# A Perceiver block on one core: first two text key tiles by plain products, bias rows in one pass, image part and last rescalings on GpSimd, last output in two pieces

## Chip, cores and metric

One core of one Trainium2 chip runs the whole block as one program. The metric is the device time of one execution in microseconds (us); smaller is better.

## What is computed

128 latent rows of width 512 go through three stages: cross attention over 12,544 context rows, self attention (16 heads of 128, weights given as 4-bit codes with scales), and a mixture of experts (2 shared, 32 routed, all computed). Only the cross attention is touched. Cut to what matters:

```python
xq = _layernorm(x)
q = rms_norm(linear(xq, q_w, q_b), norm_q_w)                 # 16 heads of 32
k_img, v_img = rms_norm(linear(ctx[:257], k_img_w, k_img_b), norm_k_img_w), linear(ctx[:257], v_img_w, v_img_b)
k_txt, v_txt = rms_norm(linear(ctx[257:], k_w, k_b), norm_k_w), linear(ctx[257:], v_w, v_b)
att = attention(q, k_img, v_img) + attention(q, k_txt, v_txt)
x1 = x + linear(att, o_w, o_b)
```

(The first lines are a summary in the reference's own function names.)

## The kernel before

**Tiling.** Keys come in tiles of 128. Group 0 is the image: 257 keys in three tiles (its last tile starts at the last image key). The text keys from 256 on make groups 1 to 24 of 512 keys, four tiles or two *pairs* each. The work runs in steps s = 0 to 26, each of 16 slots h (one per head). In step s the scores, maxima, exponentials, transposes and value products of group s-1 are interleaved with the key and value products of the next keys: slots 0 to 7 compute the second pair of group s, slots 8 to 15 the first pair of group s+1. Step 0 has the image's products (`image`) and slots 8 to 15 only.

**Products of text keys.** A pair of tiles times the K and V weights is a 2 by 2 block product. It is done with seven block products (Strassen-Winograd, `NPOS = 7`), not eight: POOL forms sums of key blocks (`first_sums`, `third_sum`, `fourth_sum`, L549 to L562) and the sums of weight blocks once (L514 to L524), and every operand is split into a high part that the one-pass float32r format holds and the low rest (`split_first`, `split`, L569 to L580 on POOL; for weights `split_weight`, high part on ACT L656 to L667, low part on DVE L924). Each block product is six one-pass matmuls of 512 columns (hi·hi, hi·lo, lo·hi for two chunks), so a pair costs 42 on PE (L1354). DVE and ACT take the sums out of PSUM. The image tiles use the plain form: 12 matmuls for a tile and a weight (L1245).

**Order.** Each engine has one queue, in the order of the code; nothing is scheduled at run time. `steps` runs each engine's `step` function. PE's score product in slot h waits for ACT's exponential of slot h-2 (`e_exp`, two score banks). ACT's `scale_keys(s, 1)` stands in slot 1 of its queue ahead of the exponential of slot 2, and waits for POOL's `key_norm(s, 1)` (L480, L482), which POOL's queue has behind all blocks of the step before and the next `first_sums(0)`. SP issues the loads, and `stack`: 12 DMAs that put transposed keys of eight heads into `k_stack`. The memset of `p_tail` on POOL waits for the eighth low weight part (`e_wlo`).

**Start.** PE spreads six bias and norm rows over 128 partitions, each by a float32 product of a row of ones with the row (L1250), four ahead of the transposes of the normalised x and two behind them; then the query product (L1264), then the image.

**End.** Steps 25 and 26 only drain (`draining`). DVE holds two running outputs, `o_st[0]` of the image and `o_st[1]` of the text. In step 24 it normalises the image's part (L987, L989) and adds two bias rows (L991, twice). In slot 12 of steps 3 to 25 it rescales `o_st[1]` (L1107), and in slot 14 adds the newest output (L1115). In step 26 ACT copies the 512 columns of the last output from PSUM (L795), PE transposes them back, DVE scales and adds (L1104, L1105, L1112, L1113), PE transposes the sum, ACT copies it (L839), and PE multiplies it with the output weight (L1437).

```python
if end and h == (5 if s >= NG else 4):
    eng.wait_ge(e_pv, (s - 2) * (NH // HC) + NH // HC)
```

## Time and profile before

| | us |
|---|---|
| median of 3 runs | 1240.7 (1240.31 to 1241.61) |
| the profiled execution | 1240.53 |
| its span, first to last instruction | 1238.8 |
| busy PE | 1186.9 (96%) |
| busy PE weight loads | 928.5 (75%) |
| busy DVE | 951.4 (77%) |
| busy ACT | 825.4 (67%) |
| busy POOL | 761.6 (61%) |

PE is TensorE, PEld its weight loads, DVE VectorE, ACT ScalarE, POOL GpSimd, SP the queue that issues DMAs. Times in rows are us from the span's start; L12 is line 12 of the kernel. A timeline row gives start, length, engine, line, operation, output <- inputs, shapes, count, and in brackets the idle time before it and what ended it. PE's matmuls overlap, so the distance of two starts is what one costs, not the length shown. PEclk is the TensorE clock granted, as a share of full speed.

### The profile page before, as it was taken

The numbers are of one execution on the slowest core, as the hardware profiler recorded it, in microseconds if no ns is written. First come the engines' busy times: TensorE is split into PE (matmuls) and PEld (weight loads), VectorE is DVE, ScalarE is ACT, GpSimd is POOL, SyncE is SP. The second block draws the span as 40 slices with busy tenths as digits, with TensorE's granted clock in tenths as the row PEclk, the third lists the DMA queues.
The fourth block names the chain that finished last, engine by engine and source line by source line (L and its number), as shares of the span: only waits on it lengthen the run. The fifth ranks groups of instructions, "written<-read, shape, count | busy, mean of one in ns | idle before, by whom it ended". The sixth has DMA issues, their size and how long they took to land.

```text
span 1238.8 us, 26287 instructions
## 1 busy us (share of the span) xinstructions
PE 1186.9 (96%) x8740; PEld 928.5 (75%) x8740; DVE 951.4 (77%) x1647; ACT 825.4 (67%) x1828; POOL 761.6 (61%) x1071
## 2 busy tenths in 40 slices
PE   8779999999999999999999999999998779899998
PEld 4557887887888788887878887887787535488886
DVE  3648888788888888887887887888877823399997
ACT  4547767777676777677767767776777713377775
POOL 5988787778787787877787877888772000000000
PEclk9989999999999999999999999999999999999999
DMA  6125866666766667656667666676653999359990
GB/s 237 31 73 137 214 166 171 163 168 187 187 171 165 170 163 213 173 161 173 171 177 195 173 162 172 156 209 174 171 136 94 290 392 362 153 222 358 363 369 21
DMA packets 132390, 236.74 MB, mean 191 GB/s; under 512 B 18081, under 2 KB 45217, under 8 KB 131873
## 3 DMA queue, kind: packets, MB, share of 16 engines
q1 hardware_dynamic: 132258, 235.06, 64.4%
q8 instruction: 73, 1.20, 0.4%
q14 instruction: 59, 0.48, 0.1%
HBM read 140.87 MB, written 17.04 MB: 127 GB/s over the span
## 4 chain that ended last, share of the span: by engine, by line
PE 82%; DVE 9%; POOL 4%; issue 3%; ACT 1%; DMA 0%; POOLq 0%; SPq 0%; DVEq 0%; ACTq 0%
PE ps L1354 31%; PE ps L1237 17%; PE ps L1420 8%; PE ps L1380 8%; PE ps L1452 3%; DVE small L1058 3%; PE ps L1532 3%; PE ps L1535 3%; PE ps L1538 3%; DVE v_second L1041 2%; DVE kt_lo L948 2%; PE ps L1553 1%; PE ps L1561 1%; PE ps L1557 1%; PE ps L1509 1%
## 5 line engine op out<-in xcount | busy, mean ns | idle before, releaser
L1354 PE MATMUL ps<-w_text,cx_blocks 128*128 128x512 f32 x2016 | 548.8, 398 | 4.5 <-ACT u_sb L773 2.0
L1354 PEld LDWEIGHTS ps<-w_text,cx_blocks 128*128 128x128 f32 x2016 | 375.0, 190 | 71.6 <-issue 4.2
L783 ACT ACTIVATE p<-ps,small 128x512 f32<-128x512 f32 (+2 forms) x400 | 271.3, 678 | 210.7 <-DVE small L1060 206.5
L1058 DVE TENSOR_REDUCE small<-ps 128x1 f32<-128x512 f32 (+2 forms) x400 | 270.7, 677 | 129.2 <-PE ps L1380 128.8
L1237 PE MATMUL ps<-ident,p 128*128 128x128 f32 x1584 | 239.7, 273 | 8.9 <-DVE pt L1051 6.9
L1237 PEld LDWEIGHTS ps<-ident,p 128*128 128x128 f32 x1584 | 194.0, 140 | 64.1 <-issue 12.7
L1380 PE MATMUL ps<-k_stack,q_stack 96*128 96x512 f32 (+1 forms) x400 | 192.1, 481 | 7.7 <-ACT p L783 7.7
L765 ACT ACTIVATE pt<-ps 128x512 f32<-128x512 f32 (+1 forms) x250 | 147.6, 590 | 11.4 <-PE ps L1237 7.0
L580 POOL TENSOR_TENSOR cx_blocks<-cx_sum,cx_blocks 128x256 fp32r<-128x256 f32 x192 | 141.7, 738 | 15.1
L578 POOL TENSOR_TENSOR cx_blocks<-cx_sum,small 128x256 fp32r<-128x256 f32 x192 | 119.6, 623 | 45.6 <-PE ps L1354 37.7
L1060 DVE TENSOR_TENSOR small<-small 128x1 f32<-128x1 f32 x400 | 130.3, 326 | 13.7
L1051 DVE COPY pt<-ps 128x512 f32<-128x512 f32 (+1 forms) x150 | 101.4, 676 | 2.2 <-PE ps L1237 2.2
L1380 PEld LDWEIGHTS ps<-k_stack,q_stack 96*128 96x128 f32 x400 | 75.7, 190 | 28.0 <-issue 20.2
L569 POOL TENSOR_TENSOR cx_blocks<-cx,small 128x512 fp32r<-128x512 f32 x48 | 51.4, 1072 | 71.7 <-PE ps L1354 71.7
L948 DVE TENSOR_TENSOR kt_lo<-ps,kt_hi 128x512 fp32r<-128x512 f32 x99 | 67.5, 682 | 27.3 <-ACT kt_hi L706 27.3
L1158 DVE TENSOR_TENSOR w_lo<-expert,w_hi 128x2048 fp32r<-128x2048 f32 x34 | 77.8, 2290 | 11.7 <-ACT w_hi L869 11.6
L701 ACT ACTIVATE kb<-kb,small 128x512 f32<-128x512 f32 x99 | 70.5, 713 | 23.7 <-POOL small L482 23.6
L490 POOL TENSOR_TENSOR codes<-codes,code_scale 128x512 f32<-128x512 f32 x64 | 82.4, 1287 | 0.1
L783 ACT ACTIVATION_READ_ACCUMULATOR p<-ps,small 128x1 f32 x400 | 77.6, 194 | 0.0
L706 ACT ACTIVATE kt_hi<-ps 128x512 fp32r<-128x512 f32 x99 | 58.9, 595 | 27.7 <-PE ps L1237 27.5
L1237 PEld LDWEIGHTS ps<-ident,kb 128*128 128x128 f32 x396 | 47.0, 141 | 31.3 <-issue 18.5
L1237 PE MATMUL ps<-ident,kb 128*128 128x128 f32 x396 | 60.6, 276 | 10.3 <-DVE kt_lo L948 6.7
(218 smaller groups left out, 1861.0 us busy)
## 6 DMA issues: line engine op xcount, KB each, us to landing
expert<-experts SPq DMA_DIRECT2D x34, 1536.0 KB, 8.6
k_stack<-kt_hi SPq DMA_DIRECT2D x384, 128.0 KB, 2.4
cx<-ctx_t SPq DMA_DIRECT2D x48, 512.0 KB, 4.2
k_stack<-kt_lo SPq DMA_DIRECT2D x192, 128.0 KB, 2.4
codes<-codes SPq DMA_DIRECT2D x64, 256.0 KB
code_scale<-code_scales SPq DMA_DIRECT2D x256, 64.0 KB
scaled<-codes SPq DMA_DIRECT2D x64, 256.0 KB, 4.3
weight_q<-scaled SPq DMA_DIRECT2D x1, 4096.0 KB, 14.2
```

The costliest lines, as they stand in the source:

```text
L578: eng.tensor_tensor(block(i, 0), of, ones.broadcast_to((P, CD, P)), ALU.mult).then_inc(e_ahi, 1)
L580: eng.tensor_tensor(block(i, 1), of, block(i, 0).bitcast(F32), ALU.subtract).then_inc(e_ab, 1)
L765: eng.activation(pt_sb[hp % NPT][:, 0:n], ps_pt[hp % 2][:, 0:n], copy).then_inc(e_pta, 1)
L783: eng.activation(pb[:, lo:hi], score_bank(s, h)[:, lo:hi], exp, bias=nm[1 - par][:, h:h + 1], accum_out=ls[1 - par][:, h:h + 1]).then_inc( ...
L948: eng.tensor_tensor(kt_lo[:, :, part], ps_t[:, :].rearrange("p (c k) -> p c k", c=DC), kt_hi[:, :, part].bitcast(F32), ALU.subtract).then_ ...
L1051: eng.tensor_copy(pt_sb[hp % NPT][:, 0:n], ps_pt[hp % 2][:, 0:n]).then_inc(e_pte, 1)
L1058: eng.tensor_reduce(ngm[:, h:h + 1], score_bank(s, h)[:, lo:hi], AX.X, ALU.max, negate=True).then_inc(e_gm, 1)
L1060: eng.tensor_tensor(nm[1 - par][:, h:h + 1], ngm[:, h:h + 1], old[:, h:h + 1], ALU.min).then_inc(e_nm, 1)
L1237: last = eng.transpose(dst[:, c * P:(c + 1) * P], src[:, c * P:(c + 1) * P], ident[:, :])
L1354: last = eng.matmul(ps_a[(p + i + 1) % 2][:, :], blk[:, i, a, c * P:(c + 1) * P], w_t[:, i, w, c * D:(c + 1) * D], start=(i in FRESH and c ...
L1380: eng.matmul(score_bank(s, h)[:, 0:n], q_st[qi][0:NST * HD, h, :], stk[0:NST * HD, h, 0:n], start=True, stop=True).then_inc(e_qk, 1)
L1420: last = eng.matmul(ps_o[jp * HD:(jp + 1) * HD, c * P:(c + 1) * P], vb[k][:, head * HD:(head + 1) * HD], pt_sb[head % NPT][:, k * P:(k + 1 ...
```

## The change

1. **Rows at the start.** The six rows lie on six partitions. POOL makes a selector of 6 by 768, ACT and DVE split the rows in high and low, and PE spreads each row by two one-pass matmuls. Three rows go ahead of the query product and three behind it. The layer norm no longer waits for the first image tile.
2. **First pair of text keys.** It is computed plainly: POOL makes only a high and a low part of the 256 keys (`pair_hi`, `pair_lo`), PE does four products of 12 matmuls (48 in place of 42). Step 0 is `image` alone, with no slots; POOL leaves out the pair's sums and seven block splits. Weights are split in another order, the two that the plain values need first (raw blocks `b12`, `b22`), and the last of nine in slot 0 of step 1. The loads of the next keys go ahead of `stack(0, True)` on SP.
3. **End.** POOL takes the image part's scaling and two additions and the rescalings of steps 24 and 25. In steps 25 and 26 ACT's copy moves from slot 5 to slot 7. The last output goes through as 384 and 128 columns.

POOL's queue from the last image split on, where the first text pair and the key norms of the image stand (`cx` are the loaded keys, `cx_sum` their sums, `cx_blocks` the split blocks, `w_sum` and `stage_k`, `stage_v` the weights, `first_pair` the new high and low part). Before:

```order
L506 TENSOR_SCALAR small<-small 128x1 [waits q_squared]
L509 TENSOR_TENSOR small<-small 128x1 [waits pool_init]
L549 TENSOR_TENSOR cx_sum_88<-cx 128x256 [waits keys_loaded0]
L553 TENSOR_TENSOR cx_sum_89<-cx_sum_88,cx 128x256 [waits key_sums]
L480 TENSOR_TENSOR small<-small 128x1 [waits k_squared]
L482 TENSOR_TENSOR small<-small 128x1 [waits k_mean_square]
L569 TENSOR_TENSOR cx_blocks<-cx,small 128x2x256
L571 TENSOR_TENSOR cx_blocks<-cx,cx_blocks 128x2x256 [waits block_hi]
L480 TENSOR_TENSOR small<-small 128x1 [waits k_squared]
L482 TENSOR_TENSOR small<-small 128x1 [waits k_mean_square]
L514 TENSOR_TENSOR w_sum_58<-stage_v,stage_k 128x1024 [waits w_loaded_v,w_loaded_k]
```

and now:

```order
L517 TENSOR_TENSOR first_pair_91<-cx,small 128x1024 [waits cx_lo,keys_loaded0]
L519 TENSOR_SCALAR small<-small 128x1 [waits q_squared]
L522 TENSOR_TENSOR small<-small 128x1 [waits pool_init]
L525 TENSOR_TENSOR first_pair_92<-cx,first_pair_91 128x1024 [waits block_hi]
L489 TENSOR_TENSOR small<-small 128x1 [waits k_squared]
L491 TENSOR_TENSOR small<-small 128x1 [waits k_mean_square]
L489 TENSOR_TENSOR small<-small 128x1 [waits k_squared]
L491 TENSOR_TENSOR small<-small 128x1 [waits k_mean_square]
L530 TENSOR_TENSOR w_sum_58<-stage_v,stage_k 128x1024 [waits w_loaded_v,w_loaded_k]
```

The two sums and two splits of the first pair are gone from between the query's and the key norms; one split of 1024 columns stands ahead of the query's two operations and one behind them. Behind the weight sums (L514 to L524, now L530 to L536 and L549) the second pair follows at once.

PE's queue behind the second transposes of the queries (L1274 before, L1349 now), up to the first score product. Before:

```order
L1274 MATMUL ps<-ident,q_thrice_121 96x128 x15
L1354 MATMUL ps<-w_text,cx_blocks 128x512 [waits v_stored,w_lo_split,block_split]
L1354 MATMUL ps<-w_text,cx_blocks 128x512 x5
L1354 MATMUL ps<-w_text,cx_blocks 128x512 [waits v_stored,w_lo_split,block_split]
L1354 MATMUL ps<-w_text,cx_blocks 128x512 x5
L1354 MATMUL ps<-w_text,cx_blocks 128x512 [waits first_product_biased,w_lo_split,block_split]
L1354 MATMUL ps<-w_text,cx_blocks 128x512 x5
L1354 MATMUL ps<-w_text,cx_blocks 128x512 [waits k_biased,w_lo_split,block_split]
L1354 MATMUL ps<-w_text,cx_blocks 128x512 x5
```

and now (each of the four products is 12 matmuls):

```order
L1349 MATMUL ps<-ident,q_thrice_126 96x128 x15
L1318 MATMUL ps<-w_text,first_pair_91 128x512 [waits v_stored,w_lo_split,block_split]
L1318 MATMUL ps<-w_text,first_pair_91 128x512
L1318 MATMUL ps<-w_text,first_pair_92 128x512
L1318 MATMUL ps<-w_text,first_pair_91 128x512 x2
L1318 MATMUL ps<-w_text,first_pair_92 128x512
L1318 MATMUL ps<-w_text,first_pair_91 128x512 x2
L1318 MATMUL ps<-w_text,first_pair_92 128x512
L1318 MATMUL ps<-w_text,first_pair_91 128x512 x2
L1318 MATMUL ps<-w_text,first_pair_92 128x512
L1318 MATMUL ps<-w_text,first_pair_91 128x512 [waits v_stored,w_lo_split]
```

The block product that waited for sums, copies and `block_split` is replaced by plain ones that wait for the low weight parts, `v_stored` and `k_biased`; the seven block products of the second pair follow, each still waiting for `block_split`.

DVE's queue in step 24, slots 12 to 14 (`small` holds maxima and sums, `o_st_111` is the image's output, `o_st_112` the text's; 116 and 117 now). Before:

```order
L1095 TENSOR_TENSOR small<-small 128x16 [waits o_added,l_added,alpha]
L1098 TENSOR_TENSOR small<-small 128x16 [waits l_scaled,exp]
L1107 TENSOR_TENSOR o_st_112<-o_st_112,small 128x512
L1058 TENSOR_REDUCE small<-ps 128x1 [waits scores]
L1060 TENSOR_TENSOR small<-small 128x1 [waits group_max]
L991 TENSOR_TENSOR o_st_111<-o_st_111,o_rows 128x512
L1058 TENSOR_REDUCE small<-ps 128x1 [waits scores,dve_chain]
L1060 TENSOR_TENSOR small<-small 128x1 [waits group_max]
L1051 COPY pt_102<-ps 128x512 [waits pv_batch,p_transposed]
L1115 TENSOR_TENSOR o_st_112<-ps,o_st_112 128x512 [waits o_scaled,o_transposed]
```

and now:

```order
L1119 COPY pt_105<-ps 128x512 [waits pv_batch,p_transposed]
L1161 TENSOR_TENSOR small<-small 128x16 [waits o_added,l_added,alpha]
L1164 TENSOR_TENSOR small<-small 128x16 [waits l_scaled,exp]
L1126 TENSOR_REDUCE small<-ps 128x1 [waits scores]
L1128 TENSOR_TENSOR small<-small 128x1 [waits group_max]
L1126 TENSOR_REDUCE small<-ps 128x1 [waits scores]
L1128 TENSOR_TENSOR small<-small 128x1 [waits group_max]
L1119 COPY pt_107<-ps 128x512 [waits pv_batch,p_transposed]
L1188 TENSOR_TENSOR o_st_117<-ps,o_st_117 128x512 [waits o_scaled,o_transposed]
```

The rescaling and one of the two bias additions between the maxima are gone from DVE; in POOL's queue they follow the last key norm. The addition of the newest output still waits for `o_scaled`.

The diff, cut to its core:

```diff
-                if s == 0:
-                    eng.wait_ge(e_klo, GT)
-                    eng.wait_ge(e_vp, GT)
-                    stack(0, True)
...
+                if s == 0:
+                    eng.wait_ge(e_klo, GT)
+                    eng.wait_ge(e_vp, GT)
+                    stack(0, True)
...
-            eng.memset(ones_row[:, :], 1.0).then_inc(e_pool, 1)
+            sel = row_ones[:, :, :]
+            eng.memset(sel, 0.0).then_inc(e_pool, 1)
             eng.memset(ident[:, :], 0.0).then_inc(e_pool, 1)
             eng.wait_ge(e_pool, 2)
+            eng.affine_select(out=sel, in_=sel, compare_op=ALU.not_equal, fill=1.0,
+                              base=0, pattern=[[-1, NROW], [0, P]], channel_multiplier=1).then_inc(e_pool, 1)
...
+                keys = cx[:, :, 0:2 * P]
+                eng.wait_ge(e_c[0], 16)
+                eng.wait_ge(e_clo, GT)
+                eng.tensor_tensor(pair_hi[:, :, :], keys, ones.broadcast_to((P, DC, 2 * P)), ALU.mult).then_inc(e_ahi, 1)
                 eng.wait_ge(e_qsq, 1)
...
+                eng.wait_ge(e_ahi, 1)
+                eng.tensor_tensor(pair_lo[:, :, :], keys, pair_hi[:, :, :].bitcast(F32), ALU.subtract).then_inc(e_ab, NPOS)
+                key_norm(0, 0, 1)
+                key_norm(0, 1, 1)
...
+            def image_part():
+                eng.wait_ge(e_orows, 48)
+                eng.wait_ge(e_irl, 1)
+                o3 = o_st[0][:, :].rearrange("p (h d) -> p h d", h=NH)
+                eng.tensor_tensor(o3, o3, rl.unsqueeze(2).broadcast_to((P, NH, HD)), ALU.mult).then_inc(e_img, 1)
+                for i in (1, 2):
+                    eng.wait_ge(e_img, i)
+                    eng.tensor_tensor(o_st[0][:, :], o_st[0][:, :], o_rows[:, i, :], ALU.add).then_inc(e_img, 1)
+
+            def last_weight_sum():
+                eng.wait_ge(e_wlo, 4)
+                eng.tensor_tensor(b12, b22, b12, ALU.subtract).then_inc(e_tt, 1)
...
-                if nxt:
+                strass = nxt and s > 0
+                if strass:
                     first_sums(0)
-                if s == 0:
-                    key_norm(0, 0, 1)
...
-                if nxt:
+                if strass:
                     split_first(0)
-                if s == 0:
...
+                    if s == 0:
+                        last_weight_sum()
                     split(1, 2, sum_y[:, :, :], 2)
-                    key_norm(s + 1, 0, 1)
+                    if s > 0:
+                        key_norm(s + 1, 0, 1)
...
+                    if s == 0:
+                        key_norm(1, 0, 1)
+                        eng.wait_ge(e_wlo, 8)
+                        eng.memset(p_tail, 0.0).then_inc(e_pz, 1)
                     split(1, 6, quarter(1, 1, 1), 0)
+                if s == NG - 1:
+                    image_part()
+                if s in (NG - 1, NG):
+                    eng.wait_ge(e_al, s - 1)
+                    eng.wait_ge(e_oadd, s - 2)
+                    o3 = o_st[1][:, :].rearrange("p (h d) -> p h d", h=NH)
+                    eng.tensor_tensor(o3, o3, al.unsqueeze(2).broadcast_to((P, NH, HD)), ALU.mult).then_inc(e_osc, 1)
```

```diff
-                        eng.wait_ge(e_qp, 1)
-                    eng.activation(w_t[:, i - 1, 0, :], (t2[:, :, :], t1[:, :, :], b12, b22, b21)[i - 3].rearrange("p c o -> p (c o)"),
+                    if i == 8:
+                        eng.wait_ge(e_pp, NPOS)
+                    if i > 4:
+                        eng.wait_ge(e_tt, (2, 1, 4, 3)[i - 5])
+                    eng.activation(w_t[:, W_SLOT[i - 3], 0, :], (b12, b22, t2[:, :, :], t1[:, :, :], b12, b21)[i - 3].rearrange("p c o -> p (c o)"),
...
-            for i in range(4):
-                store_row(i)
+            eng.wait_ge(e_pool, 4)
+            eng.activation(row_sel[:, :, :], row_ones[:, :, :], copy).then_inc(e_rowh, 1)
...
+            eng.activation(row_hi[:, :], row_sb[:, :], copy).then_inc(e_rowh, 1)
+            store_row(0)
+            store_row(1)
...
+            def plain_values(j):
+
+                eng.wait_ge(*((e_pp, NPOS) if j else (e_vp, GT + 1)))
+                eng.activation(v_first[1][j][:, :], ps_a[0][:, :], copy).then_inc(e_v, 1)
...
                     image()
+                    plain_values(0)
+                    square_keys(1, 0, 1)
+                    plain_values(1)
+                    scale_keys(1, 0, 1)
+                    split_weight(8)
+                    return
...
-                    if end and h == (5 if s >= NG else 4):
-                        eng.wait_ge(e_pv, (s - 2) * (NH // HC) + NH // HC)
...
+                        if s <= NG:
+                            eng.activation(ot_sb[:, :], ps_o[:, :], copy).then_inc(e_oc, 1)
+                        else:
+                            eng.activation(ot_sb[:, 0:TA], ps_o[:, 0:TA], copy).then_inc(e_oc, 1)
+                            eng.wait_ge(e_pv, NG * (NH // HC))
+                            eng.activation(ot_sb[:, TA:], ps_s[0][:, 0:P], copy).then_inc(e_oc, 1)
```

```diff
-                    if not loop and s == NG - 1:
-                        image_part(h)
+                    if s == NG - 1 and h == 8:
+                        eng.reciprocal(rl, l_st[0]).then_inc(e_irl, 1)
...
-                        else:
+                        elif s < NG - 1:
                             eng.tensor_tensor(o3, o3, al.unsqueeze(2).broadcast_to((P, NH, HD)), ALU.mult).then_inc(e_osc, 1)
...
+                            for i, (src, part) in enumerate(((ps_t[:, 0:TA], slice(0, TA)), (ps_s[1][:, 0:P], slice(TA, D)))):
+                                n = (part.stop - part.start) // HD
+                                heads = rl[:, part.start // HD:part.stop // HD].unsqueeze(2).broadcast_to((P, n, HD))
+                                dst = o_st[0][:, part]
+                                eng.wait_ge(e_ot, NG + i)
+                                chain(eng.tensor_tensor(dst.rearrange("p (h d) -> p h d", h=n), src.rearrange("p (h d) -> p h d", h=n),
+                                                        heads, ALU.mult))
+                                eng.tensor_tensor(dst, dst, o_st[1][:, part], ALU.add).then_inc(e_osum, 1)
...
-                eng.matmul(ROW_BANKS[i][:, :], ones_row[:, :], row_sb[:, i * D:(i + 1) * D], start=True, stop=True).then_inc(e_row, 1)
...
+                eng.matmul(ROW_BANKS[i][:, :], row_sel[:, i, :], row_hi[:, :], start=True, stop=False)
+                eng.matmul(ROW_BANKS[i][:, :], row_sel[:, i, :], row_lo[:, :], start=False, stop=True).then_inc(e_row, 1)
+
+            eng.wait_ge(e_pool, 4)
+            eng.wait_ge(e_rowh, 2)
+            eng.wait_ge(e_rowo, 1)
+            spread_row(0)
+            spread_row(1)
...
+            spread_row(2)
...
+            for i in range(3, NROW):
+                spread_row(i)
...
+                eng.wait_ge(e_ab, NPOS)
+                for j in range(2):
+                    keys = slice(j * P, (j + 1) * P)
+                    a = [(pair_hi[:, c, keys], pair_lo[:, c, keys]) for c in range(DC)]
+                    for of, at in (("k", (0, 1)), ("v", (6, 5))):
+                        eng.wait_ge(e_wlo, 3 if of == "k" else 5)
+                        if of == "k":
+                            eng.wait_ge(*((e_kb, GT + 1) if j else (e_v, 2)))
+                        else:
+                            eng.wait_ge(e_v, GT + j)
+                        w = [(w_t[:, at[c // CD], 0, c % CD * D:(c % CD + 1) * D],
+                              w_t[:, at[c // CD], 1, c % CD * D:(c % CD + 1) * D]) for c in range(DC)]
+                        last = split_product(ps_a[of == "k"][:, :], a, w, 0, 3 * DC)
+                        if of == "k" or j == 0:
+                            last.then_inc(e_kp if of == "k" else e_vp, 1)
+                last.then_inc(e_pp, NPOS)
...
+                    if s == 1 and p < 0 and i in (2, 3, 4, 6):
+                        eng.wait_ge(e_wlo, 9 if i == 6 else i + 4)
...
+                        into = ps_s[0][:, 0:P] if s == NG + 1 and c == TA // P else ps_o[:, c * P:(c + 1) * P]
+                        if s == NG + 1 and c == TA // P:
+                            eng.wait_ge(e_oc, NG)
+                            transposes(ps_t, ot_sb, TA // P).then_inc(e_ot, 1)
...
+                    if end and h == 12 and s == NG + 1:
+                        eng.wait_ge(e_oc, NG + 1)
+                        eng.transpose(ps_s[1][:, 0:P], ot_sb[:, TA:], ident[:, :]).then_inc(e_ot, 1)
...
-            transposes(ps_t, o_st[0]).then_inc(e_at, 1)
-            eng.wait_ge(e_atc, 1)
+            transposes(ps_t, o_st[0], TA // P).then_inc(e_at, 1)
+            eng.wait_ge(e_osum, 2)
+            eng.transpose(ps_s[0][:, 0:P], o_st[0][:, TA:], ident[:, :]).then_inc(e_at, 1)
...
+                eng.wait_ge(e_atc, 1 if c < TA // P else 2)
```

## Rows read from the trace of the kernel before

**Rows 1.** Stretches: length, busy (count) of PE PEld DVE ACT POOL; PEclk, DMA, GB/s
```profile
20.00:70.00 50.00, 41.19 (x195) 31.47 (x193) 34.38 (x42) 23.73 (x44) 44.44 (x43) 1.00 0.22 60
70.00:80.00 10.00, 3.06 (x10) 2.62 (x11) 1.42 (x4) 4.44 (x13) 9.36 (x15) 0.59 0.16 52
80.00:90.00 10.00, 10.00 (x75) 8.04 (x73) 6.46 (x15) 6.21 (x17) 8.47 (x14) 0.90 0.02 3
```

**Rows 2.** Timeline of PE, first and fifth score product of step 1
```profile
61.52 0.28 PE L1380 MATMUL ps<-k_stack,q_stack 96*128 96x258 f32 x1
...
76.94 0.58 PE L1380 MATMUL ps<-k_stack,q_stack 96*128 96x258 f32 x1 [7.21 <-ACT p L783]
```

**Rows 3.** Timeline of ACT, the operation that held PE
```profile
75.10 0.72 ACT L701 ACTIVATE kb<-kb,small 128x512 f32<-128x512 f32 x1 [8.28 <-POOL small L482]
```

**Rows 4.** Timeline of POOL, from the query's scale to the key norm of step 1
```profile
23.45 1.40 POOL L506 TENSOR_SCALAR small<-small 128x1 f32<-128x1 f32 x1 [6.35 <-ACT q_sq L721]
...
25.46 0.74 POOL L549 TENSOR_TENSOR cx_sum<-cx 128x256 f32<-128x256 f32 x1
...
32.81 2.55 POOL L514 TENSOR_TENSOR w_sum<-stage_v,stage_k 128x1024 f32<-128x1024 f32 x1
...
35.65 2.62 POOL L482 TENSOR_TENSOR small<-small 128x1 f32<-128x1 f32 x1
...
64.49 0.95 POOL L622 MEMSET p_tail<- 128x1020 f32 x1
...
74.52 0.55 POOL L482 TENSOR_TENSOR small<-small 128x1 f32<-128x1 f32 x1
```

**Rows 5.** POOL's work on tile cx_blocks, 25.4 to 59.9 us: length, busy (count)
```profile
25.40:59.90 34.50, 13.06 (x12) 1.00 0.10 24
```

**Rows 6.** Groups of POOL there, the sums: count | busy us, mean ns | idle before
```profile
L553 POOL TENSOR_TENSOR cx_sum<-cx_sum,cx 128x256 f32<-128x256 f32 x2 | 1.8, 902 | 0.2
L562 POOL TENSOR_TENSOR cx_sum<-cx,cx_sum 128x256 f32<-128x256 f32 x1 | 1.7, 1719 | 0.0
L558 POOL TENSOR_TENSOR cx_sum<-cx 128x256 f32<-128x256 f32 x1 | 1.6, 1605 | 0.1
```

**Rows 7.** Timeline of DVE, the low part of the text key weights
```profile
35.58 2.28 DVE L924 TENSOR_TENSOR w_text<-stage_k,w_text 128x2048 fp32r<-128x2048 f32 x1
```

**Rows 8.** Timeline of PE, from rows and query product to second query transposes
```profile
3.89 7.16 PE L1250 MATMUL ps<-rows,ones_row 1*128 1x512 f32 x8 [3.89 <-DMA rows<-first_rows]
...
15.74 6.07 PE L1264 MATMUL ps<-wq,pt 128*128 128x512 f32 x8
21.25 0.80 PE L1245 MATMUL ps<-w_hi_k_img,img_cx_hi 128*128 128x512 f32 x1
...
29.84 0.60 PE L1237 MATMUL ps<-ident,kb 128*128 128x128 f32 x4
...
45.09 1.91 PE L1274 MATMUL ps<-ident,q_thrice 128*96 128x128 f32 x16
```

**Rows 9.** Timeline of SP, the issue of the first weight
```profile
2.60 0.51 SPq L320 DMA_DIRECT2D stage_k_img<-k_img_wt  x1
```

**Rows 10.** DMA issues, the same load: KB, us from issue to landing
```profile
stage_k_img<-k_img_wt SPq DMA_DIRECT2D x1, 1024.0 KB, 8.2
```

**Rows 11.** Timeline of DVE, step 24: one that goes, two that stay
```profile
957.02 0.68 DVE L989 TENSOR_TENSOR o_st<-o_st,small 128x512 f32<-128x512 f32 x1
...
968.36 0.68 DVE L1058 TENSOR_REDUCE small<-ps 128x1 f32<-128x512 f32 x1
969.08 0.74 DVE L1060 TENSOR_TENSOR small<-small 128x1 f32<-128x1 f32 x1
```

**Rows 12.** Timeline of POOL, its one addition in that stretch
```profile
968.52 1.28 POOL L634 TENSOR_TENSOR x_again<-x_again,o_rows 128x512 f32<-128x512 f32 x1 [14.63 <-DMA x_again<-x]
```

**Rows 13.** Timeline of DVE, the last sum
```profile
996.91 0.69 DVE L1113 TENSOR_TENSOR o_st<-o_st,o_st 128x512 f32<-128x512 f32 x1
```

**Rows 14.** Timeline of PE, the output product
```profile
999.00 3.70 PE L1437 MATMUL ps<-wo,kb 128*128 128x512 f32 x8 [0.69 <-ACT kb L839]
```

185 lines of the change are left out of this document (94 added, 91 removed).

## Prediction

> **What bounds the kernel now.** I read the page first (PE busy for 96% of the span), then the chain of waits, then the busy time in stretches, then the timelines of the stretches where PE is not full. Three quarters of the execution is steps 1 to 24 with PE always busy; the change leaves them alone, so they only move. What it can win lies in the first 80 us, in the drain (steps 24 to 26) and in the last output.
>
> At the start one place stands out. PE issues the first score product of step 1 at 61.52 and the fifth at 76.94, after 7.21 us of idleness [rows 2]. It waits for ACT's exponential, ACT stands in its queue at the key scaling of step 1, and that has waited 8.28 us for POOL's key norm [rows 3], whose last operation starts at 74.52 [rows 4]. POOL is busy for 9.36 of 10 us there while PE has 3.06 [rows 1]. So POOL's queue sets when step 1 can go on, and the length of that queue is what the change cuts. The idle PE also loses its clock: granted 0.59 in 70 to 80 us and 0.90 in 80 to 90 us [rows 1].
>
> **POOL's queue.** Removed for the first pair: 12 instructions on the blocks, 13.06 us [rows 5], and the four sums of 0.74, 0.90, 1.60 and 1.72 us [rows 4, 6], 18.0 us together; with some 0.07 us between neighbours 19 us. Added: high and low part of 1024 columns. The nearest row from above is a weight sum of 1024 columns, 2.55 us [rows 4]; from below twice nothing, if both fall into idle time. The high part stands in the 6.35 us in which POOL waited for the query [rows 4] and is free; I take 2.5 us for the low part. The query is squared earlier (below), so the scaling that started at 23.45 starts at about 19, 4.3 us earlier. Sum: 74.5 - 19 - 4.3 + 2.5 = 53.7 for the last key norm, were POOL's queue all there is. It now also waits: the memset of `p_tail` stands behind the eighth low weight part on DVE. Behind the memset come its own 0.95 us [rows 4], one split (1.4), two sums (1.6) and the norm (0.8), for which see the next paragraph.
>
> **PE's own queue becomes the bound.** Rows at the start: eight records of 7.16 us [rows 8] ahead of the transposes, and two rows more behind them, turn into four one-pass matmuls ahead, two behind and six after the query product. A one-pass matmul of 512 columns costs 8.59 / 36 = 0.24 us (36 of them from 21.25 to 29.84 [rows 8]), so 12 cost 2.9 us. The new work ahead of it is not shown by any row: POOL makes a selector of 768 columns on six partitions twice, ACT and DVE copy and subtract. By the memset of 1020 columns at 0.95 [rows 4] this is 0.7 us for each of POOL's two, at most 1.7 for the selection, and 1 to 2 us on ACT and DVE; I put the rows at 6.6 and the query product at 9.9, not 15.74 [rows 8]. It takes 5.5 us (15.74 to 21.25), three rows 1.4 us: image products from 16.8. The other bound of that moment is the first weight: issued at 2.60, 8.2 us to landing [rows 9, 10], so 10.8, then 1.8 us on ACT and 2.3 us on DVE (2048 columns take 2.28 [rows 7]): 15.0. So 16.8, between 15.2 and 17.8, where it was 21.25.
>
> From there PE has 36 + 36 image and 48 plain matmuls (six more than the pair's 42, 1.4 us of PE), that is 120 x 0.24 = 28.7 us, three groups of key transposes at 0.44 (29.84, four of them), and two of 16 query transposes at 1.9 at most [rows 8]: 33.8 us. That gives 50.6; for the waits that are left (third key tile, which needs ACT, POOL and DVE in turn) 0.4: step 1 starts at 51.0 instead of 61.52. Slots 0 to 3 took 76.94 - 7.21 - 61.52 = 8.2 us [rows 2]; they have a ninth weight split on ACT and DVE beside them now. So the fifth score product is at 59.2.
>
> POOL is then not late: the eighth low part follows DVE's use of the third plain product (48.1), at 50.5; memset, split, sums and norm make 55.1, or 56.7 if DVE's ninth split holds POOL up; ACT's scaling, squares and exponential then allow the fifth product at 57.2 to 58.8. The two paths are within 2 us, which is why I don't count on less than 59. The 12 DMAs of the second `stack` may start at 51 and are needed by ACT in slot 5, some 10 us later: covered, with 1 us to spare.
>
> The fifth product moves from 76.94 to 59.2: **17.7 us**. And PE, now without a gap of 7 us, keeps the full clock. The clock has two levels, 1.2 and 2.4 GHz; a mean of 0.59 is 8.2 us at the lower, with nearly all of PE's 3.06 us in it, and 0.90 is 2 us [rows 1]. Half of that work time is lost: 1.5 + 1.0; I take **2.3 us**.
>
> **Drain.** In step 24 DVE is busy without pause. It loses one scaling, two additions and a rescaling, in step 25 another rescaling, 0.68 us each [rows 11]: 3.4 us. POOL has the time: its only work there is one addition of 1.28 us [rows 12], so four make 5.3 us from slot 8, and the addition of slot 14 finds its rescaling ready. But POOL's work costs DVE something. DVE's minimum of two one-column operands takes 0.16 us at 968.36 and 0.74 at 969.08 [rows 11], when POOL's addition ran from 968.52 to 969.80 [rows 12]: it ended with it. Such a minimum stands behind every maximum. Five new POOL operations at 0.58 us each: 2.9 us back. Net 0.5.
>
> The Trainium skill (SBUF — State Buffer, the part on the shared port pair) says that a DVE instruction with two SBUF inputs and a GpSimd instruction that reads SBUF exclude each other for their whole length. The row at 969.08 agrees; taken at its worst, every POOL operation would hold DVE for all of its length, which is a rival below.
>
> ACT's copy in slot 7 instead of 5 lets two exponentials of step 25 go first: 0.3.
>
> **Last output.** The first 384 columns go ahead, but DVE reaches them only after the same work as before, so the first sum ends at about 997.1, not 997.6 (996.91 + 0.69 [rows 13]). Transposes and copy of three quarters are each 0.1 to 0.2 shorter, and the last quarter hides behind the first three chunks of the product. That starts at 998.3 instead of 999.00 [rows 14]: 0.7. Nothing later changes.
>
> **Sum.** 17.7 + 2.3 + 0.5 + 0.3 + 0.7 = 21.5 us. Against the profiled execution (1240.53, span 1238.8) this gives 1219.0; the median of the runs is 1240.7, so the two bases are one for this purpose. A measurement of this kernel can tell 0.2%, 2.5 us, from no change.
>
> **Rivals.**
> 1. *POOL stays the bound.* For it: a sum of 256 columns took 0.74 us alone and 1.60 and 1.72 beside DVE's splits [rows 4, 6], a norm 2.62 beside a split from 35.58 [rows 4, 7]. If five operations more are stretched by 0.9, the fifth product is at 63.7: 1223.5. Against it: DVE's splits then fall where POOL would wait anyway. Chance 0.20.
> 2. *No cost on DVE, fewer waits.* The weight bounds the image at 15.2, the third key tile costs nothing, and the drain gives the whole 3.4 us: 1.6 + 2.4 = 4 us more, 1215. Chance 0.20.
> 3. *POOL holds DVE at its worst in the drain.* Five operations at 1.28 are 6.4 us against 3.4: 3.5 us worse than my 0.5, 1222.5. Chance 0.07.
> 4. *Slower: PE runs the new start at 1.2 GHz.* At half clock each us of PE time loses half a us; the 21.5 us are gone when 43 us of the start, nearly all of 17 to 60, run so. Then 120 matmuls and the transposes cost 34 us more: 1253. Against it: from 20 to 70 us the granted clock was 1.00, with PE idle for 9 of the 50 us [rows 1]. Chance 0.02.
> 5. *The POOL stop was not what held step 1*, the weights' low parts were, and the ninth comes no earlier than the last did: within 0.2%. Against it: 8.28 us at one wait [rows 3]. Chance 0.01.
>
> The forecast itself has 0.50. Its range, with start and end bounds, is 1216 to 1222; to hold eight in ten I reach to rivals 1 to 3 and some way beyond: 1213 to 1225. Faster by over 0.2%: 0.97; within: 0.01; slower: 0.02.
>
> **What would show it.** Image products start near 17; step 1's first score near 51 and its fifth near 59; the granted clock stays at 1 from 10 to 90 us; DVE's minima in step 24 average over 0.4 us; the output product starts 0.7 us closer to the last value product. I am wrong if ACT's key scaling of step 1 again waits over 3 us for POOL, if PE's steps 1 to 23 get another length, or if the drain from step 24 on changes by over 3 us.

## The result, and the profile after

The changed kernel takes 1229.24 us, the median of 4 runs (1228.29 to 1230.93), the kernel before 1241.15 us beside it: ratio 0.990, 95% interval 0.9886 to 0.9913. That is 11.9 us faster. Forecast were 1219.0 us and a range of 1213 to 1225: the sign is right, the gain is half of what was forecast, and the time lies outside the range. The profiled execution took 1228.65 us, its span 1226.9, so it can be compared with the one before (1240.53, 1238.8).

Where TensorE's timeline stands at the same instruction in both:

| instruction | before | after | won so far |
|---|---|---|---|
| first score product of step 1 | 61.52 | 59.17 | 2.35 |
| fifth score product of step 1 | 76.94 | 68.85 | 8.09 |
| first of step 2 | 103.96 | 95.25 | 8.71 |
| first of step 24 | 952.95 | 944.74 | 8.21 |
| last value product | 994.16 | 984.55 | 9.61 |
| output product | 999.00 | 988.45 | 10.55 |
| first expert product | 1084.00 | 1073.17 | 10.83 |
| last product | 1234.96 | 1223.08 | 11.88 |

The stretches that answer to [rows 1], same columns:

```profile
20.00:70.00 50.00, 41.16 (x195) 32.66 (x194) 36.53 (x41) 28.07 (x53) 46.97 (x42) 0.97 0.27 76
70.00:80.00 10.00, 9.91 (x78) 7.75 (x76) 6.96 (x16) 7.34 (x20) 9.16 (x15) 1.00 0.03 10
80.00:90.00 10.00, 8.87 (x70) 6.69 (x69) 6.10 (x14) 6.09 (x17) 6.64 (x11) 1.00 0.48 121
```

The hole of 70 to 80 us is gone, and the clock is 1.00 there. But POOL is busy for 46.97 of the 50 us from 20 on, more than before, although 16 instructions of the first pair have left its queue and only two have come. TensorE's timeline says where the early lead went (first image product, first key transposes, then the first and the fifth score, which answer to [rows 2]):

```profile
17.79 0.50 PE L1318 MATMUL ps<-w_hi_k_img,img_cx_hi 128*128 128x512 f32 x1 [0.30 <-DVE w_lo_k_img L983]
...
31.29 1.05 PE L1310 MATMUL ps<-ident,kb 128*128 128x128 f32 x4 [4.98 <-ACT kb L739]
32.14 3.20 PE L1349 MATMUL ps<-ident,q_thrice 128*96 128x128 f32 x16
...
59.17 0.28 PE L1473 MATMUL ps<-k_stack,q_stack 96*128 96x258 f32 x1
...
68.85 0.39 PE L1473 MATMUL ps<-k_stack,q_stack 96*128 96x258 f32 x1 [0.52 <-ACT p L835]
```

The image products start 3.5 us earlier than before, yet the first key transposes start 1.5 us later (29.84 before [rows 8]), after a wait of 4.98 us, and the 16 query transposes behind them take 3.20 instead of 1.91 us: the clock had gone down to its lower level (granted 0.83 on the mean of 30 to 40 us, 1.00 before). The cause stands in the timelines of POOL and DVE:

```profile
14.54 1.04 POOL L511 TENSOR_TENSOR img_cx_hi<-img_cx,small 128x512 fp32r<-128x512 f32 x1 [5.70 <-DMA img_cx<-ctx_t]
15.66 3.22 POOL L513 TENSOR_TENSOR img_cx_lo<-img_cx,img_cx_hi 128x512 fp32r<-128x512 f32 x1
18.85 1.03 POOL L511 TENSOR_TENSOR img_cx_hi<-img_cx,small 128x512 fp32r<-128x512 f32 x1
20.03 3.16 POOL L513 TENSOR_TENSOR img_cx_lo<-img_cx,img_cx_hi 128x512 fp32r<-128x512 f32 x1
23.33 1.89 POOL L517 TENSOR_TENSOR first_pair<-cx,small 128x1024 fp32r<-128x1024 f32 x1
25.31 0.19 POOL L519 TENSOR_SCALAR small<-small 128x1 f32<-128x1 f32 x1
25.59 0.56 POOL L522 TENSOR_TENSOR small<-small 128x1 f32<-128x1 f32 x1
26.10 2.34 POOL L525 TENSOR_TENSOR first_pair<-cx,first_pair 128x1024 fp32r<-128x1024 f32 x1
...
66.15 0.20 POOL L489 TENSOR_TENSOR small<-small 128x1 f32<-128x1 f32 x1
66.43 0.55 POOL L491 TENSOR_TENSOR small<-small 128x1 f32<-128x1 f32 x1
```

```profile
15.00 2.73 DVE L983 TENSOR_TENSOR w_lo_k_img<-stage_k_img,w_hi_k_img 128x2048 fp32r<-128x2048 f32 x1 [7.28 <-ACT w_hi_k_img L686]
...
19.16 2.88 DVE L983 TENSOR_TENSOR w_lo_v_img<-stage_v_img,w_hi_v_img 128x2048 fp32r<-128x2048 f32 x1 [0.83 <-ACT w_hi_v_img L686]
21.96 0.68 DVE L1020 TENSOR_TENSOR kb<-ps,k_bias 128x512 f32<-128x512 f32 x1
```

The image's low parts took POOL 1.26 us before and take 3.22 and 3.16 now: the first weights are ready sooner, so DVE's low parts fall on them. POOL is through with the image at 23.2, then makes the pair's high part, and the query's scale, which was to start at 19, starts at 25.31. The norm that the fifth score needs starts at 66.15; it was 74.25 before. The fifth score stands 2.7 us behind this start in both. The sign that I had named for a POOL that is still the bound did not come, though: ScalarE's key scaling waits 1.00 us for POOL, not over 3.

```profile
67.01 0.73 ACT L739 ACTIVATE kb<-kb,small 128x512 f32<-128x512 f32 x1 [1.00 <-POOL small L491]
```

That wait is short because TensorE and ScalarE are late themselves: the first score of step 1 stands at 59.17 and not at 51.0.

### The profile page after: what moved, and what is told of

Same layout as the page of the kernel before. It is cut to its first block, busy times and chain, and to the rows that moved or that the text cites. A ratio compares the mean times of both kernels' runs of the same rounds, so it can differ in the third digit from the quotient of the medians.

```text
span 1226.9 us, 26290 instructions
## 1 busy us (share of the span) xinstructions
PE 1179.2 (96%) x8746; PEld 925.8 (75%) x8746; DVE 954.3 (78%) x1643; ACT 827.7 (67%) x1833; POOL 764.6 (62%) x1063
## 4 chain that ended last, share of the span: by engine, by line
PE 80%; DVE 9%; POOL 5%; issue 3%; DMA 1%; ACT 1%; SPq 0%; POOLq 0%; DVEq 0%; ACTq 0%
PE ps L1447 31%; PE ps L1310 16%; PE ps L1517 8%; PE ps L1473 8%; PE ps L1554 4%; DVE small L1126 3%; PE ps L1634 3%; PE ps L1637 3%; PE ps L1640 3%; DVE v_second L1109 2%; DVE kt_lo L1012 2%; PE ps L1655 1%; PE ps L1663 1%; PE ps L1659 1%; PE ps L1611 1%
## 5 line engine op out<-in xcount | busy, mean ns | idle before, releaser
L1447 PE MATMUL ps<-w_text,cx_blocks 128*128 128x512 f32 x1974 | 536.8, 397 | 1.3 <-ACT v_first L792 0.7
L1447 PEld LDWEIGHTS ps<-w_text,cx_blocks 128*128 128x128 f32 x1974 | 366.4, 189 | 65.7 <-issue 2.7
L605 POOL TENSOR_TENSOR cx_blocks<-cx_sum,cx_blocks 128x256 fp32r<-128x256 f32 x188 | 138.8, 738 | 14.8
L1128 DVE TENSOR_TENSOR small<-small 128x1 f32<-128x1 f32 x400 | 132.8, 332 | 13.7
L1012 DVE TENSOR_TENSOR kt_lo<-ps,kt_hi 128x512 fp32r<-128x512 f32 x99 | 67.5, 682 | 25.4 <-ACT kt_hi L744 25.2
```

Of the source, the lines that this page charges most:

```text
L605: eng.tensor_tensor(block(i, 1), of, block(i, 0).bitcast(F32), ALU.subtract).then_inc(e_ab, 1)
L1012: eng.tensor_tensor(kt_lo[:, :, part], ps_t[:, :].rearrange("p (c k) -> p c k", c=DC), kt_hi[:, :, part].bitcast(F32), ALU.subtract).then_ ...
L1128: eng.tensor_tensor(nm[1 - par][:, h:h + 1], ngm[:, h:h + 1], old[:, h:h + 1], ALU.min).then_inc(e_nm, 1)
L1447: last = eng.matmul(ps_a[(p + i + 1) % 2][:, :], blk[:, i, a, c * P:(c + 1) * P], w_t[:, i, w, c * D:(c + 1) * D], start=(i in FRESH and c ...
```

## The experiments

There are two theories for the 9.6 us that the start fell short (fifth score at 68.85, forecast 59.2). **Order**: instructions of the first pair stand ahead of the query's scale and the key norms. **Turns**: GpSimd's instructions and DVE's instructions with two SBUF inputs run one after the other, so only their sum counts. One measure serves throughout, the **chain**: from POOL's start on the second image tile (14.54 above) to the start of that norm (66.15), 51.6 us; it was 61.9 before (12.31 to 74.25). Each run below has one profile. How far the chain can be trusted is shown by the six profiles whose start is that of the changed kernel (the changed kernel, 1, 11, 12, 14, 15): 51.6 or 51.7 us in all six. In the two with the old start it is 61.9 and 60.9 (before, 2).

**1. The start alone** (image part, rescalings, last output and copy as before):

```diff
-                if s == NG - 1:
-                    image_part()
-                if s in (NG - 1, NG):
...
+                    if not loop and s == NG - 1:
+                        image_part(h)
```

> The changed kernel with its end as before: image part and last rescalings back on DVE, the last output in one piece, ACT's copy back in slot 5. Theory: the parts add, and the start alone is worth what the trace shows between the first scores and step 24 (8.2 us, first score of step 24 at 952.95 before and 944.74 after). So 1241.2 - 8.2 = 1233.0, within 1 us, with the fifth score of step 1 near 68.9. Rival: the start is worth less by itself because the later clock return ahead of the experts (1.5 us at 1075 in the changed kernel) came with it or not by chance; then 1231.5 to 1233. If the drain terms had no worth at all it would be 1229.2.

1232.70 us, ratio 0.9923 (0.9903 to 0.9944), fifth score at 68.21, chain 51.7. By the ratio the start is worth 9.6 us (7.0 to 12.1); by this trace against the one before 8.7 at the fifth score and 9.3 at the first score of step 2. It is most of the gain.

**2. The end alone**, on the kernel before (the same lines the other way round):

> The kernel before with only the end of the change: image part and last rescalings on GpSimd, the last output in two pieces, ACT's copy in slot 7. Theory from the two traces: drain 1.4 us and last output 0.9 us, 2.3 us in all: 1238.8. My recorded forecast for these parts was 0.5 + 0.3 + 0.7 = 1.5: 1239.6. Rival, that the clock's earlier return ahead of the experts belongs to the new end and not to chance: 3.7 us, 1237.4. Rival, GpSimd holds DVE at its worst: no faster than 1241.

1240.02 us, ratio 0.9984 (0.9972 to 0.9996): 2.0 us (0.5 to 3.5). Start and end, 9.6 and 2.0, add to what the whole change gives, 11.9. But this trace has neither the short drain nor the early clock of the changed kernel's profiled execution: 40.96 us from step 24's first score to the last value product, against 39.81.

**3. and 4. Another order in GpSimd's queue.** In 3 the query's scale goes ahead of the pair's high part; in 4 the first key norm does too, and the second ahead of the low part:

```diff
-                eng.tensor_tensor(pair_hi[:, :, :], keys, ones.broadcast_to((P, DC, 2 * P)), ALU.mult).then_inc(e_ahi, 1)
                 eng.wait_ge(e_qsq, 1)
...
+                key_norm(0, 0, 1)
+                eng.tensor_tensor(pair_hi[:, :, :], keys, ones.broadcast_to((P, DC, 2 * P)), ALU.mult).then_inc(e_ahi, 1)
+                key_norm(0, 1, 1)
                 eng.wait_ge(e_ahi, 1)
```

> The changed kernel with the query's scale ahead of the pair's high part in GpSimd's queue, nothing else. Theory 'order': the scale starts at 23.3 instead of 25.31, DVE's normed query and the image's second and third key sums go 2 us earlier, but the first key norm stays behind the pair's low part at 28.4, so the first key transposes gain only the 0.9 us of ACT's squares; the second and third gain about 2: step 1's first score 1 to 2 us earlier, 1227.5 to 1228.2 against 1229.2. Rival 'GpSimd is full': it is busy from 14.5 to 60.9 but for 0.94 us, so an exchange within it moves nothing: 1229.2.

> The changed kernel with query scale, then first key norm, then the pair's high part, second key norm, and the pair's low part after it. Theory 'order': first key norm at about 24.7, first key transposes at 26 to 27 instead of 31.29, PE without its 4.98 us gap and without the fall of the clock to 0.83 in 30 to 40 us; step 1's first score 3 to 5 us earlier (54 to 56), whole time 1224.5 to 1226.5. Rival 'GpSimd is full': the first score comes earlier but the fifth stays at 68 to 69, because the splits of the second pair and the norm of step 1 stand at the end of GpSimd's queue: 1229.

1230.87 us (0.9915, 0.9895 to 0.9934) and 1231.09 us (0.991, 0.9893 to 0.9927). In 4 the wait that I took for the culprit is gone:

```profile
26.57 0.63 PE L1309 MATMUL ps<-ident,kb 128*128 128x128 f32 x4
...
31.30 0.63 PE L1309 MATMUL ps<-ident,kb 128*128 128x128 f32 x4 [2.35 <-DVE kt_lo L1011]
...
38.89 0.63 PE L1309 MATMUL ps<-ident,kb 128*128 128x128 f32 x4 [4.20 <-DVE kt_lo L1011]
```

TensorE reaches these transposes 4.7 us earlier and without a wait, and then waits 2.35 and 4.20 us for the next key tiles. The fifth score is at 68.24 (68.39 in 3), the chain is 51.7 (51.8): nothing won, since the second image tile was also taken up 0.6 us earlier than in the changed kernel. The theory of the order falls.

**5. More of GpSimd's work**: the pair's high part twice.

```diff
+                eng.tensor_tensor(pair_hi[:, :, :], keys, ones.broadcast_to((P, DC, 2 * P)), ALU.mult).then_inc(e_again, 1)
+                eng.wait_ge(e_again, 1)
                 eng.tensor_tensor(pair_hi[:, :, :], keys, ones.broadcast_to((P, DC, 2 * P)), ALU.mult).then_inc(e_ahi, 1)
```

> The changed kernel with the high part of the first pair made twice on GpSimd, one after the other (1024 columns, 1.89 us in the changed kernel); nothing else. Theory 'GpSimd is full': it is busy from 14.5 to 60.9, so the second copy moves the key norm that the fifth score of step 1 waits for, and this score, by 1.9 us: 51.6 us from the start of the second image tile's high part to that norm become 53.5, and the time 1231.1 against 1229.2. Rival 'the fifth score is bound by TensorE's own products, or by the weights' low parts on DVE': no change, 1229.2.

1230.73 us (0.9906, 0.9891 to 0.9921). Chain 53.6: two us longer, as the turns want. The fifth score itself is at 68.91, where it was, because POOL took up the second image tile at 12.58, two us earlier than in the changed kernel's profile. Only the chain shows the effect; the times differ by less than their intervals.

**6. Less of it**: query and norms first, the pair's high part no longer on GpSimd but on ScalarE, behind the first key squares.

```diff
                 square_keys(0, *IMAGE_TILES[0])
+                eng.activation(pair_hi[:, :, :], cx[:, :, 0:2 * P], copy).then_inc(e_ahi, 1)
                 eng.wait_ge(e_sq, 1)
```

> Like the experiment with the norms first, but the pair's high part made by ScalarE behind the first key squares (1024 columns there take 1.06 us), so GpSimd loses an instruction that took 1.89 us in the changed kernel and 3.49 us with the norms first. Theory 'GpSimd is full': the fifth score of step 1 comes 2 to 3.5 us earlier, 51.6 us from the second image tile to the norm become 48 to 49.7, the time 1226 to 1227.5. Rival 'TensorE or DVE is next': the fifth score moves by less than 1 us.

1227.41 us (0.9876, 0.9859 to 0.9892). Chain 49.7, fifth score at 66.78.

**7. The image's columns ahead of the first weight** in SP's queue:

```diff
+            eng.dma_start(img_cx[:, :, P:IT * P], cxt[:, :, P:IT * P]).then_inc(e_cx, 16)
             load_weight(0)
-            eng.dma_start(img_cx[:, :, P:IT * P], cxt[:, :, P:IT * P]).then_inc(e_cx, 16)
```

> The changed kernel with the rest of the image's columns loaded ahead of the first weight (one DMA issue moved up by one). GpSimd's second image tile starts at 14.5 in the changed kernel, when these columns land; they now land about 2.5 us earlier, the first weight 1.3 us later. Theory 'GpSimd is full and its chain starts with this landing': the chain starts near 12, and the two low parts of 3.2 us lie ahead of DVE's first low part and take 1.3: GpSimd done with the image near 17.5 instead of 23.2, then held by the query's squares at 20 to 21; the fifth score 2 to 4 us earlier, 1225 to 1227. Rival 'the first weight is the start of the chain': everything 1.3 us later, 1230.5.

POOL starts on the second tile at 9.93, and the fifth score is at 64.29, 4.6 us earlier. ScalarE takes up the first weight at 12.65, within the scatter of the other runs. The chain is 51.7 again. That is strange at first: the image's low parts take 1.26 us now, so 3.9 us of stretch are gone, and POOL waited 2.13 us for a load. The two engines show why the sum stays (DVE, then POOL):

```profile
17.40 3.48 DVE L983 TENSOR_TENSOR w_lo_v_img<-stage_v_img,w_hi_v_img 128x2048 fp32r<-128x2048 f32 x1
...
21.61 2.89 DVE L1029 SCALAR_TENSOR_TENSOR q_normed<-q_biased,small,q_rows 128x512 f32<-128x512 f32 x1
```

```profile
16.85 1.89 POOL L517 TENSOR_TENSOR first_pair<-cx,small 128x1024 fp32r<-128x1024 f32 x1 [2.13 <-DMA cx<-ctx_t]
18.82 2.11 POOL L519 TENSOR_SCALAR small<-small 128x1 f32<-128x1 f32 x1
21.02 0.56 POOL L522 TENSOR_TENSOR small<-small 128x1 f32<-128x1 f32 x1
21.54 2.41 POOL L525 TENSOR_TENSOR first_pair<-cx,first_pair 128x1024 fp32r<-128x1024 f32 x1
```

DVE's instruction starts at 17.40, stands until POOL's ends at 18.74, and then needs 2.14 us; POOL's next, of 0.19 us, stands until DVE's ends at 20.88; DVE's `q_normed`, 0.74 us where nothing runs beside it, ends 0.5 us behind the 2.41 us of POOL's low part. Neither runs slowly: each waits for the whole of the other. The measured time was 1230.45 us (0.9898, 0.9882 to 0.9915), no better than the changed kernel: see 11 and 13.

**8. Image columns first, with 6's order and high part on ScalarE:**

```diff
+            eng.dma_start(img_cx[:, :, P:IT * P], cxt[:, :, P:IT * P]).then_inc(e_cx, 16)
             load_weight(0)
...
                 square_keys(0, *IMAGE_TILES[0])
+                eng.activation(pair_hi[:, :, :], cx[:, :, 0:2 * P], copy).then_inc(e_ahi, 1)
```

> Both: image columns ahead of the first weight, query scale and key norms ahead of the pair's parts, the high part on ScalarE. If GpSimd's queue is the bound in both, the gains add: 4 to 7 us, 1222 to 1225. If TensorE's queue takes over (120 products of 0.24 us and 5.1 us of transposes from 19 on give a first score near 53), the first score is at 53 to 55, the fifth at 62 to 64, 1223 to 1224. Rival 'DVE's low parts take over', eight of 1024 columns behind ScalarE: less than 2 us, over 1227.

1227.60 us (0.9884, 0.9869 to 0.9898), fifth score at 65.09, later than in 7. The gains do not add: with less work GpSimd now waits, 3.70 us for the squares of the query and 2.08 and 1.14 for those of the keys, and the chain is 52.2. The turns bind only while both engines have work.

**9. More of DVE's work and none of GpSimd's**: the low part of the third weight twice, at a place where DVE waits anyway. This is the run that tells turns from a full queue.

```diff
+                if i == 2:
+                    eng.tensor_tensor(dst, whole, high.bitcast(F32), ALU.subtract).then_inc(e_again, 1)
+                    eng.wait_ge(e_again, 1)
                 eng.tensor_tensor(dst, whole, high.bitcast(F32), ALU.subtract).then_inc(e_wlo, 1)
```

> The changed kernel with the low part of the third weight (2048 columns, 2.3 us when nothing else runs) made twice on DVE, one after the other, at 34 us, where DVE then waits 2.08 us for ScalarE; GpSimd's instructions are untouched. Theory 'GpSimd and DVE take turns': GpSimd's instructions alone (34.4 us at their shortest) and DVE's with two SBUF inputs (18.2 us) add to the 51.6 us from the second image tile to the key norm of step 1, so 2.3 us more on DVE make 53.9 of 51.6, the fifth score comes 2.3 us later after the landing, time 1231.5. Rival 'only GpSimd's own queue counts' or DVE's idle time takes it: 51.6 stays, 1229.2.

1231.92 us (0.9922, 0.9907 to 0.9937), chain 53.5. DVE and POOL around it:

```profile
31.82 2.59 DVE L984 TENSOR_TENSOR w_text<-stage_k,w_text 128x2048 fp32r<-128x2048 f32 x1
34.44 2.29 DVE L986 TENSOR_TENSOR w_text<-stage_k,w_text 128x2048 fp32r<-128x2048 f32 x1
38.47 0.69 DVE L1015 TENSOR_TENSOR kt_lo<-ps,kt_hi 128x512 fp32r<-128x512 f32 x1 [1.74 <-ACT kt_hi L744]
```

```profile
32.22 2.24 POOL L489 TENSOR_TENSOR small<-small 128x1 f32<-128x1 f32 x1
34.60 2.54 POOL L491 TENSOR_TENSOR small<-small 128x1 f32<-128x1 f32 x1
```

DVE still waits 1.74 us afterwards, so its own queue had room for the second low part; POOL's step of 0.55 us takes 2.54. The 2.3 us that DVE got lengthen the chain by 1.9. As in 5, the fifth score is where it was, at 68.61, because the chain began two us earlier (12.39).

**10. The better start**: image columns first, the high part on ScalarE right behind the second image weight.

```diff
                 split_weight(1)
+                eng.wait_ge(e_clo, GT)
+                eng.wait_ge(e_c[0], 16)
+                eng.activation(pair_hi[:, :, :], cx[:, :, 0:2 * P], copy).then_inc(e_ahi, 1)
                 eng.wait_ge(e_qb, 1)
```

> The changed kernel with the image's columns loaded ahead of the first weight, and the pair's high part on ScalarE behind the second image weight's (so GpSimd's queue is query scale, low part, norms and sums as in the changed kernel). By the turns theory 1.9 us of GpSimd's work leave the chain while DVE's two low parts of 2.3 us run in GpSimd's idle time: 1 to 2 us better than with the image first alone, whose fifth score was at 64.29: 62.4 to 63.3, first score near 54. Time 1224 to 1226.5 if the end is as in most runs. Rival 'TensorE is next': the third key tile still waits, fifth score at 64.

1226.74 us (0.9883, 0.9866 to 0.99), first score at 53.26, fifth at 62.95, chain 50.5: 1.1 us shorter than in 7, where 1.9 us of work left. GpSimd waits 4.25 us for the query's squares here.

**11. TensorE kept busy in three waits of the end**, by transposes whose result nobody reads:

```diff
+            def fill(n):
+                for _ in range(n):
+                    eng.transpose(ps_a[1][:, 0:P], ident[:, :], ident[:, :])
...
+            fill(8)
             eng.wait_ge(e_osum, 1)
...
+            fill(24)
             eng.wait_ge(e_ln, 1)
```

> The changed kernel with 56 more transposes of the identity into a free PSUM bank: 8 where TensorE waits 1.3 us ahead of the last output's transposes, 24 in each of the two waits of 3.3 and 3.2 us ahead of the self-attention and ahead of the gate. No data depend on them. Theory 'the last 8 us of scatter between executions are TensorE's clock, which falls when it has been idle': the granted clock then stays at 1.00 from the output product to the experts, the output product always takes 3.7 us and the part from the gate to the end 151.2 or less, 1.5 to 3 us gained: 1226.5 to 1228, with less scatter. Rival 'the clock falls by something else than idleness': unchanged, 1229.2.

1227.87 us (0.9882, 0.9868 to 0.9897). From the output product to the experts the granted clock is 1.00 throughout, and so it is in 13, 14 and 15, which have these transposes too. In the stretches 980:1000 and 1060:1080 it was 0.93 and 0.91 in the changed kernel:

```profile
980.00:1000.00 20.00, 16.57 (x133) 10.54 (x134) 6.61 (x16) 3.76 (x10) 1.09 (x6) 1.00 1.04 395
1000.00:1020.00 20.00, 20.00 (x54) 9.19 (x53) 4.15 (x6) 1.19 (x2) 0.00 (x0) 1.00 1.05 391
1060.00:1080.00 20.00, 18.30 (x86) 12.78 (x85) 10.94 (x33) 8.44 (x11) 0.74 (x2) 1.00 0.00 1
```

From the last value product to the last product it takes 236.1 us; the changed kernel took 238.5 in its profiled execution. In five of the 13 executions profiled without these transposes (1, 4, 6, 7, 12) the granted clock between the output product and the first projection was 0.65 to 0.87, and this part took 9.3 to 11.4 us instead of 8.3. Run 7 was one of them, with 11.43. That is where 3 of its 4.6 us went in that execution.

**12. Image part and rescalings back on DVE**, the last output still in two pieces; **14. the same, with the idle transposes of 11. 15. With these transposes too, but with image part and rescalings on GpSimd and the last output in one piece, with the copy in slot 5.** The first diff belongs to 12 and 14, the second to 15.

```diff
-                            eng.wait_ge(e_img, 3)
...
-                        elif s < NG - 1:
+                        else:
                             eng.tensor_tensor(o3, o3, al.unsqueeze(2).broadcast_to((P, NH, HD)), ALU.mult).then_inc(e_osc, 1)
```

```diff
-            transposes(ps_t, o_st[0], TA // P).then_inc(e_at, 1)
-            eng.wait_ge(e_osum, 2)
-            eng.transpose(ps_s[0][:, 0:P], o_st[0][:, TA:], ident[:, :]).then_inc(e_at, 1)
+            transposes(ps_t, o_st[0]).then_inc(e_at, 1)
```

> The changed kernel with image part and the last rescalings back on DVE (as in the kernel before), the last output still in two pieces. Theory from the traces so far: step 24's first score to the last value product took 41.2 us before and 40.6 to 41.0 us in the runs with this part on GpSimd (39.8 once), so this part is worth 0 to 0.5 us: 1229.2 to 1229.7. My recorded forecast gave it 0.5. Rival, it is worth the whole 3.4 us of DVE's work: 1232.6.

> The changed kernel with the idle transposes and with image part and last rescalings back on DVE; to be read against the kernel with the idle transposes alone (1227.9), where the clock no longer differs between executions after the last value product. Theory 'this part is worth about half a us': 1228.0 to 1228.8, and step 24's first score to the last value product 41.0 to 41.5 us against 40.94. Rival 'worth 2 us or more, as the medians 1232.1 and 1232.7 of the two kernels with it on DVE suggest': 1230 or over.

> The changed kernel with the idle transposes and with the last output in one piece and ScalarE's copy in slot 5, as before; to be read against the kernel with the idle transposes alone (1227.9). Last value product to output product took 4.84 and 4.85 us in the two profiles with one piece and 3.90 in most with two: 0.9 us, so 1228.8. Rival 'the two pieces also change the drain before them': over 1229.5 or under 1228.3.

1232.09 us (0.9921, 0.9904 to 0.9937), 1225.94 (0.9873, 0.9856 to 0.989) and 1226.97 (0.9884, 0.9867 to 0.9901). Against 11 (0.9882) both 14 and 15 are no slower, where 0.5 and 0.9 us slower were expected, and all intervals overlap: by the runs alone the two end parts are worth less than these runs can tell. The traces tell more, if executions with the same granted clock are compared. From step 24's first score to the output product, at a mean clock of 0.96 up to the last value product:

| | us |
|---|---|
| rescalings on DVE, one piece (before, 1) | 46.05, 45.76 |
| rescalings on DVE, two pieces (12, 14) | 45.35, 45.36 |
| rescalings on GpSimd, two pieces (2, 3, 5, 8, 11) | 44.86, 44.65, 44.82, 44.51, 44.84 |

Run 6 belongs to the last row by its clock up to the last value product, but the clock was 0.82 behind it: 45.21. So each of the two parts is worth about 0.6 us. One more pair says so of the last output: at a clock of 1.00 up to the output product, one piece took 44.41 us (15) and two pieces 43.71 (the changed kernel's profiled execution). At 0.92 (4, 7, 9, 10, 13) the part up to the last value product alone takes 41.9 to 42.3 us instead of 39.81.

**13. 10 and 11 together:**

> The two versions that did better, together: image columns first with the pair's high part on ScalarE, and the 56 idle transposes. The first acts up to step 2 (5.9 us at the fifth score), the second from the last value product on (2.4 us against the changed kernel's profiled execution, which had a good clock there; 3 to 5 against most others), so they should add: 1229.2 - 5.5 - 2.5 = 1221 to 1223. Rival 'the clock takes back at the end what was won at the start', whatever stands there: not under 1225.

1223.79 us (1221.43 to 1224.33), ratio 0.9852 (0.9835 to 0.9869): 18 us faster than before and some 5.5 faster than the changed kernel. This interval lies wholly below the changed kernel's (0.9886 to 0.9913). A gain at the start does reach the end.

## Why the prediction was half right

**What failed: GpSimd's queue.** I took 13.06 and 4.96 us out of it for the first pair, the durations that the rows show. A good part of these was GpSimd standing still for DVE, and that does not leave with the instruction: DVE's work stays, and the next instruction of GpSimd stands for it. Counted at the shortest duration of their form in these traces (2.34 and 1.26 us for a low part of 1024 and 512 columns, 0.73 for one of 256 and for a sum; 1.89, 1.04 and 0.61 for a high part), the 16 instructions are 12.0 us, not 18. The two that came are 1.89 + 2.34 = 4.2, where I had 2.5: the high part was costed at nothing, in a wait of 6.35 us that had gone, since the image's columns landed at 14.5 and not 12.3, its low parts stood 3.9 us for DVE, and the query was sooner. In the terms of the forecast: the last operation of the norm was to start at 53.7 and started at 66.43. Of these 12.7 us, 6.1 stand ahead of the query's scale (25.31 in place of 19.2) and 6.6 behind it (41.1 us from there in place of 34.5). For the whole chain the same count gives:

| | GpSimd, shortest | DVE, two SBUF inputs | sum | chain |
|---|---|---|---|---|
| before | 42.0 | 17.4 | 59.4 | 61.9 |
| after | 34.4 | 18.2 | 52.6 | 51.6 |

The change took 7.6 us out of GpSimd's work and put 0.8 on DVE, and the remaining 3.5 us are waits of GpSimd for others that are gone (it waited 6.35 us for the query before, in part beside DVE's work, and 0.94 us in all now). The chain is as short as the sum allows. That the sum is 1.0 us over it is not explained: no run shows what overlaps. The chain is 10.3 us shorter and starts 2.2 us later: the 8.1 us won at the fifth score. Runs 5, 6 and 9 add or take about 2 us on either engine and find them in the chain; runs 3 and 4 exchange and find nothing. The times alone would not show this, since the intervals of 5, 6, 9 and 10 all overlap the changed kernel's; the evidence is the chain, which differs by under 0.1 us between six profiles of the same start. Rival 1 (POOL stays the bound, 0.20) was the right mechanism with a price of 4.5 us instead of 9.6, and the argument that I set against it, that DVE's splits would fall where POOL waits anyway, was wrong for want of such waits. The Trainium skill (SBUF — State Buffer, the part on the shared port pair) says that whichever of the two starts first holds the pair for its whole instruction and the other fully blocks. I quoted it for the drain and let it price nothing at the start; the rows of 7 agree with it within 0.2 us.

**TensorE's queue.** Query product at 10.27 (forecast 9.9), first image product at 17.79 (16.8, bounds 15.2 to 17.8): the first weight, which landed at 10.8 before, was taken up by ScalarE at 13.06. With an unchanged order of loads that moment lies between 10.9 and 13.1 in eleven profiles, and the image's columns are taken up between 12.4 and 14.5: the landing I built on, 10.8, lies ahead of all of them. Step 1's first score came at 59.17, not 51.0: the waits of 4.98, 0.91 and 0.62 us are 6.5 us where I had 0.4, the image products began 1.0 us late, and the transposes behind the first wait ran at the lower clock. Slots 0 to 3 took 9.7 us, not 8.2.

**The clock at the start**: 0.6 us of the 2.3. The stretch 70 to 90 us is at 1.00 as forecast, but TensorE waits there for 1.1 us, and the statement that it stays at 1 from 10 us on was wrong: the wait ahead of the key transposes brought a new fall (0.83 in 30 to 40 us).

**Drain and last output.** 0.8 and 0.7 forecast, 1.5 us; 1.2 measured at the same clock, and 2.3 between the two profiled executions, one of which had the full clock. For the rescalings the forecast was 0.5 and the runs show 0.6, but this is luck and not the working. The cost on DVE was overrated: its 24 minima from step 24's first score to the last value product take 5.8 to 6.3 us (changed kernel, 2, 11) against 4.3 to 4.4 (before, 1, 12), so 1.4 to 2 us came back and not 2.9; in step 24 they average 0.29 us, not over 0.4. Of the 3.4 us taken from DVE, 1.4 to 2 should then have been left by my working. That only 0.6 reached TensorE means that DVE was not the bound all the way; what was is not shown.

**"Nothing later changes"** held for the work, not for the time: 1.3 us more come between output product and end. No instruction was changed there; the clock came back sooner ahead of the experts (1076 after 1072, against 1089 after 1082). In this pair of executions the change's own work is 8.7 + 1.2 = 9.9 us; of the other 2, 1.1 and 1.3 are clock and -0.5 is a scatter of steps 2 to 23, which differ by up to 1.3 us between these runs. The pair has luck on both sides. The changed kernel's profile has the latest landing of the image's columns of all eleven (14.54) and the one before an early one (12.31; 14.22 in 2): on the mean of the six profiles with the new start and the two with the old one, the fifth score came 9.2 us earlier and the first of step 2 9.9. Against that, no other profile without idle transposes has a clock as good at the end. The two roughly cancel: 9.9 + 1.2 = 11.1 us is near the 11.9 of the medians.

## What to carry to other kernels

- Before taking an instruction's duration out of a queue, ask how much of it was waiting for another engine. For GpSimd beside DVE add up GpSimd's work and DVE's work with two SBUF inputs, each at its shortest; if the sum fills the chain, an exchange within a queue wins nothing, and only work moved to a third engine does (6 and 10 here), and that until one of them waits for something else (8).
- Name a sign of being wrong that the rival can't avoid. Mine was one long wait; the rival came as holds inside many instructions and as waits at other places, and the sign stayed silent.
- When a change removes the reason why one start was late, look for the load that is next, and in how many profiles it lands when.
- Compare the parts of two profiles at the same granted clock. A late gain or loss in code that was not touched may be the clock: look there first. Cheap idle work on TensorE in a known wait held it here.

## What the runs showed of the hardware that was not expected

- DVE's instructions with two SBUF inputs and GpSimd's that read SBUF shut each other out for their whole length, in both directions. An instruction of GpSimd on a single column, 0.19 us, took 2.11 us behind a low part on DVE; DVE's multiply of 512 columns, 0.74 us, took 2.8 to 2.9 us behind a low part on GpSimd. DVE's instructions of 512 columns with one input in PSUM are not held: such an addition took 0.68 us at 21.96, while GpSimd's low part was running to 23.19, and 0.67 to 0.69 us in all profiles up to 110 us.
- The clock's state at the end differs between executions, here single profiles of kernels whose code is the same from there on: 39.8 to 42.3 us for the drain with GpSimd's rescalings and two pieces, 8.3 to 11.4 from the output product to the first projection, 149.9 to 151.3 from the first expert product to the last. With the idle transposes the last two are 8.3 to 8.4 and 149.5 to 150.4, and 2.1 us go off the stretch from the first projection to the experts; the drain, where there are none, still differs (granted 0.92 to 1.00).
- The same DMAs in the same order land up to 2 us apart from one execution to the next (the image's columns are taken up between 12.4 and 14.5 us in eleven profiles), and with the new start the fifth score of step 1 follows one for one: 54.3 us behind this moment in the six profiles of that start.
